# Shorter algebra at the two row ends, seven half-units kept, and a reload moved behind the last unit

## The reference

```python
# _gn: group norm, 32 groups of 16 channels, for each batch b and group g
x0 = x
v = (x - mean_group) / sqrt(var_group + 1e-5)
y1 = depthwise_conv(v, w1)            # w1 is H x 1: one value per (b, c, column), [b, c, 1, W]
y2 = depthwise_conv(v, w2)            # w2 is 1 x W: one value per (b, c, row),    [b, c, H, 1]
xl1 = relu(batchnorm(y1) * g1 + b1)   # mean and variance over both batches and the 256 values
xl2 = relu(batchnorm(y2) * g2 + b2)
dot[c, b] = sum_k xl1[b, c, k] * xl2[b, c, k]
num = dot.reshape(b, c)               # (512, 2) read as (2, 512): row 0 comes from channels 0..255
num = softmax((num @ lw1.T + lb1) @ lw2.T + lb2)
return x0 + v * num[:, :, None, None]
```

## Time and profile before

| what | value |
|---|---|
| median of 3 runs | 1709.55 us (1707.28 to 1709.72) |
| profiled execution: time | 1705.58 us |
| profiled execution: span | 1703.8 us |
| PE, DVE, ACT, POOL busy | 28%, 59%, 39%, 30% |
| DMA | 723.80 MB, mean 425 GB/s |
| HBM | 454.63 MB read, 268.44 MB written |

### The profile page before, as it was taken

The page is one execution under the profiler, slowest core; times in us unless marked ns, Lnnn a source line. Parts: engine busy times, 40 slices in busy tenths (PEclk is TensorE's granted clock), DMA queues, the critical chain, the costliest instruction groups (busy, mean ns, idle before and its releaser), DMA issues.

```text
span 1703.8 us, 14430 instructions
## 1 busy us (share of the span) xinstructions
PE 485.6 (28%) x3416; PEld 169.7 (10%) x3416; DVE 1004.7 (59%) x2672; ACT 665.1 (39%) x517; POOL 508.9 (30%) x489
## 2 busy tenths in 40 slices
PE   3588766660223321223333243430000000000000
PEld 1123212120001100001001021210000000000000
DVE  5899999967757576776666786772222222222220
ACT  4688887856435455544445546600000000000000
POOL 7678787820315444443254000000000000000000
PEclk8799878885666665666566566665555555555555
DMA  9999999989999999999999999999999999999999
GB/s 393 426 425 427 427 428 426 428 338 419 432 428 431 431 430 431 430 432 430 432 430 430 431 428 430 430 385 431 431 432 431 432 431 431 432 431 432 431 431 408
DMA packets 52126, 723.80 MB, mean 425 GB/s; under 512 B 6241, under 2 KB 6753, under 8 KB 8034
## 3 DMA queue, kind: packets, MB, share of 16 engines
q1 hardware_dynamic: 33922, 458.84, 63.4%
q10 hardware_dynamic: 18144, 264.25, 36.3%
HBM read 454.63 MB, written 268.44 MB: 424 GB/s over the span
## 4 chain that ended last, share of the span: by engine, by line
DMA 39%; another core or an unknown queue 26%; DVE 8%; PE 3%; issue 2%; ACT 2%; SPq 1%; DVEq 1%; POOL 0%; ACTq 0%; POOLq 0%
DMA xs<-in_x 28%; DMA out<-xs 11%; DVE xs L1104 3%; PE ps_part L576 2%; DVE xs L1028 1%; DVE mul_junk L1002 1%; DVE y2s L1031 1%; SPq L378 1%; ACT xs L878 1%; PE ps_part L710 1%; ACT sq_junk L805 1%; DVEq L1002 0%; DVE xs L1002 0%; POOL rstd_b L468 0%
## 5 line engine op out<-in xcount | busy, mean ns | idle before, releaser
L805 ACT ACTIVATE sq_junk<-xs 128x4096 fp8e5<-128x4096 f32 x128 | 463.1, 3618 | 203.9 <-DMA xs<-in_x 198.6
L576 PE MATMUL ps_part<-xs,filters 128*32 128x512 f32 x1856 | 290.8, 781 | 525.3 <-DMA xs<-in_x 516.2
L1104 DVE TENSOR_SCALAR xs<-xs,scale,shift 128x4096 f32<-128x4096 f32 x90 | 222.8, 2496 | 353.9 <-DMA xs<-in_x 353.3
L1002 DVE SCALAR_TENSOR_TENSOR xs<-xs,ps_w 128x256 f32 (+1 forms) x832 | 294.5, 416 | 28.6 <-DMA xs<-in_x 18.4
L534 POOL TENSOR_TENSOR xs<-xs,w_late 128x2048 f32<-128x2048 f32 x40 | 179.6, 4526 | 102.6 <-ACT w_late L819 102.6
L878 ACT ACTIVATE xs<-xs,shift,scale 128x4096 f32<-128x4096 f32 x33 | 125.3, 3798 | 157.3 <-DVE xs L1104 135.5
L576 PEld LDWEIGHTS ps_part<-xs,filters 128*32 128x32 f32 x1856 | 79.3, 138 | 718.3 <-issue 718.3
L1028 DVE TENSOR_TENSOR xs<-xs,ps_w 128x4096 f32<-128x4096 f32 x26 | 114.7, 4413 | 52.8 <-PE ps_part L576 46.6
L468 POOL TENSOR_TENSOR rstd_b<-var,minus_half 128x2 f32<-128x2 f32 (+1 forms) x23 | 15.2, 661 | 417.2 <-DVE var L1054 417.2
L1022 DVE TENSOR_REDUCE y2s<-xs 128x8 f32<-128x2048 f32 x40 | 91.4, 2286 | 77.1 <-POOL xs L534 77.1
L439 POOL TENSOR_TENSOR xs<-xs 128x768 f32<-128x768 f32 x64 | 116.7, 1827 | 58.0 <-DMA xs<-in_x 55.0
(11 more groups left out here) (116 smaller groups left out, 458.4 us busy)
## 6 DMA issues: line engine op xcount, KB each, us to landing
xs<-in_x SPq DMA_DIRECT2D x209, 2048.0 KB, 24.0
out<-xs ACTq DMA_DIRECT2D x121, 2048.0 KB, 27.6
filters<-in_x SPq DMA_DIRECT2D x5, 2048.0 KB, 18.0
out<-filters ACTq DMA_DIRECT2D x5, 2048.0 KB, 86.2
xs<-in_lw SPq DMA_DIRECT2D x2, 2048.0 KB, 16.3
out<-xs SPq DMA_DIRECT2D x2, 2048.0 KB, 12.1
filters<-in_w_rows SPq DMA_DIRECT2D x1, 512.0 KB, 3.8
filters<-in_w SPq DMA_DIRECT2D x1, 512.0 KB, 8.9
```

Source lines behind the costliest of these rows:

```text
L576: last = nc.tensor.matmul(ps_part[g % 2][32 * a:32 * a + 32, :], taps[:, g % 2, hf * JH + j, :], xs[:, s[0]:s[1] + 1:s[1] - s[0], j * W:(j ...
L805: nc.scalar.activation(sq_junk[:], xs[:, s, :], ACT.Square, accum_out=sq_sum[:, u % 2, u // 2, b:b + 1], saturate=False).then_inc(squared, 1)
L1002: return nc.vector.scalar_tensor_tensor(out=out, in0=x_row, scalar=1.0, in1=ps_w2[g % 2][:, 0:W], op0=ALU.mult, op1=ALU.mult, accum_out=total)
L1104: return nc.vector.tensor_scalar(buffer(s), buffer(s), scale[:, b, g:g + 1], shift[:, b, g:g + 1], ALU.mult, ALU.add)
```

## The change

It has six parts.

- (a) `HELD` goes from 6 to 7: seven half-units of batch 1 stay in SBUF, and 57 are read again. Unit 57 of batch 1 moves to slot 8.
- (b) The 28 reloads of batch 0 are handed out anew: steps 38, 43 and 48 get two, steps 55, 56, 59 and 61 none, and the last is loaded behind the last unit (slot 3) and scaled by ACT behind the last store of its batch.
- (c) The order of slots in stage 4 is 8, 9, 2, 6, 7, 4, 5, then FILTERS, 0, 1, 3, so the load into FILTERS stands first. It now also waits for the rows of the last half-unit, since DVE's rows of group 31, batch 1, write their unused output there (without waits between sets).
- (d) At the row ends, the last quad: `normalise`, `channel_moments`, `channel_factors` and `rectify` are replaced by `last_quad`, which takes moments of the raw sums for each batch and forms one scale and one shift from them with small DVE operations and two POOL powers (one of which runs beside the moments). One ACT pass makes the first factor, DVE makes the second, and the logits start with batch 0's dots.
- (e) The softmax: PE adds the logits into all 128 partitions at once (its weights are the dots, broadcast), so exponential and sum are made in every partition and the four transposes, the mask and the spreading product go.
- (f) In the last group before the first row end PE convolves each batch by itself; at both row ends `turn_rows` takes three of its four groups ahead of the last half-units; the moments come ahead of the fold; `keep_warm` is 6 in one piece instead of 3 and 2. POOL waits for the coefficients before it builds the next filters.

```diff
-HELD = 6
+HELD = 7
-REWORK_AT = list(range(FIRST + 1, UNITS - 6)) + [UNITS - 5, UNITS - 3]
+TWICE = (FIRST + 6, FIRST + 11, FIRST + 16)
+REWORK_AT = sorted([*range(FIRST + 1, UNITS - 9), *TWICE, UNITS - 7])
 def rework_slot(r):
-    if r < REWORK - 4:
+    if r < REWORK - 2:
         return (2, 3, 8)[(r - 2) % 3]
-    return (3, 8, 3, 8)[r - REWORK + 4]
+    return 3
 def last_slot(i):
-    return (9, 2, 6, 7, 4, 5, 3, 8, 0, 1, FILTERS)[i % S]
+    return (8, 9, 2, 6, 7, 4, 5, FILTERS, 0, 1, 3)[i % S]
...
+            load_again(REWORK - 1)              # SP, behind the last x load
             for i in range(HELD, UNITS):
...
                 elif s == FILTERS:
                     sp.wait_ge(pe_read_x, filters_before(UNITS - 1, 1))
+                    sp.wait_ge(rows_done, rows_before(UNITS - 1, 1) + SETS)
...
             def finish_row(row):
                 q = FQ * (row + 1) - 1
+                moments(batch_of(QG * (q + 1) - 1, 1))
                 fold_parts(QG * (q + 1) - 1)
-                moments(batch_of(QG * (q + 1) - 1, 1))
-                turn_rows(q)
-                pe.wait_ge(bn_ready, q + 1)
-                keep_warm(3)
+                turn_rows(q, range(QG - 1, QG))
+                keep_warm(6)
                 add_logits(q)
-                keep_warm(2)
-                spread_prob(row)
...
+            def rectify_last(row):
+                act.wait_ge(joint_ready, row + 1)
+                for b in range(B):
+                    half = slice(b * W, (b + 1) * W)
+                    nc.scalar.activation(z[:, half], ps_y1[:, half], ACT.Relu, scale=z_scale[:, 0, b:b + 1],
+                                         bias=z_shift[:, 0, b:b + 1]).then_inc(z_done, 2)
...
+                elif b and g == G - 1:          # DVE rows of group 31, batch 1
+                    for j in range(JH):
+                        last = row(last_junk[:, j], xs[:, s, j * W:(j + 1) * W], sums[:, j:j + 1])
+                    last.then_inc(rows_done, SETS)
...
+            def last_quad(row):
+                group_moments(k)                                    # then POOL: own_rstd = var ** -0.5
+                ...                                                 # own_off, 1 operation
+                    for b in range(B):
+                        last = nc.vector.bn_stats(bn_st2[:, B * i + b], y[:, b * W:(b + 1) * W])
+                ...                                                 # 4 bn_aggr, 10 operations of 2 or 4 columns
+                                               op0=ALU.add, op1=ALU.add).then_inc(spread_ready, 1)
+                ...                                                 # POOL: var_r = var_s ** -0.5, then 4 small operations
+                last.then_inc(joint_ready, 1)
+                for b in range(B):
+                    nc.vector.tensor_scalar(ps_y2[:, halves[b]], ps_y2[:, halves[b]], z_scale[:, 1, b:b + 1],
+                                            z_shift[:, 1, b:b + 1], ALU.mult, ALU.add).then_inc(y2_scaled, 1)
+                for b in range(B):
+                    nc.vector.scalar_tensor_tensor(
+                        out=z[:, halves[b]], in0=ps_y2[:, halves[b]], scalar=0.0, in1=z[:, halves[b]],
+                        op0=ALU.max, op1=ALU.mult, accum_out=dots[:, q, b:b + 1]).then_inc(dots_ready, 1)
...
             def softmax(row):
                 dve.wait_ge(logits_ready, row + 1)
-                nc.vector.reduce_max(neg_max[:], ps_l[0:1, :], AX.X, negate=True).then_inc(exp_asked, 1)
+                nc.vector.tensor_tensor(by_group, ps_l[:].rearrange("p (g c) -> p g c", c=CG),
+                                        own[:].unsqueeze(1).to_broadcast([P, G, CG]), ALU.mult)
+                nc.vector.reduce_max(neg_max[:], ps_l[:], AX.X, negate=True).then_inc(exp_asked, 1)
+                nc.vector.tensor_reduce(logit_g[:], by_group, AX.X, ALU.add).then_inc(logits_taken, 1)
                 dve.wait_ge(exp_done, row + 1)
...
             copy_parts(FG - 1)
-            normalise(FQ - 1)
-            rectify(FQ - 1)
+            rectify_last(0)
             exponential(0)
...
-            normalise(Q - 1)
-            rectify(Q - 1)
+            rework(REWORK - 1)
+            rectify_last(1)
             exponential(1)
```

More of the change, by code:

```diff
@@ L570, in convolve @@
                     if g >= 2:
-                        pe.wait_ge(part_copied, 2 * (g - 1))
+                        pe.wait_ge(part_copied, 2 * g if g in (FG - 1, FG) else 2 * (g - 1))
+                if u == FIRST - 1:
+                    turn_rows(FQ - 1, range(QG - 1))
+                if g == FG - 1:
+                    for b in range(B):
+                        pe.wait_ge(x_loaded[s[b]], landed(s[b], ("x", u, b)))
+                        for j in range(JH):
+                            a = j % 4
+                            last = nc.tensor.matmul(
+                                ps_part[b][32 * a:32 * a + 32, 0:W], taps[:, g % 2, hf * JH + j, :],
+                                xs[:, s[b], j * W:(j + 1) * W],
+                                start=(hf == 0 and j < 4), stop=(hf == 1 and j >= JH - 4))
+                    last.then_inc(pe_read_x, 1)
+                    return
                 for b in range(B):
@@ L614, in turn_rows @@
                 for e in range(E):
-                    for a in range(QG):
+                    for a in groups:
                         last = nc.tensor.matmul(
@@ L618, in turn_rows @@
                             sel[:, q % 2, e, :], y2s[:, (QG * q + a) % (2 * QG)], start=True, stop=True)
-                last.then_inc(y2_turned, 1)
+                if groups[-1] == QG - 1:
+                    last.then_inc(y2_turned, 1)
             def moments(k):
@@ L689, in add_logits @@
                         pe.wait_ge(exp_done, row)
-                    nc.tensor.matmul(ps_l[0:1, :], one[:], bias[:], start=True, stop=False)
-                pe.wait_ge(dots_ready, 2 * (q + 1))
+                        pe.wait_ge(logits_taken, row)
+                    nc.tensor.matmul(ps_l[:], one[:].to_broadcast([1, P]), bias[:], start=True, stop=False)
                 for b in range(B):
-                    last = nc.tensor.matmul(ps_l[0:1, :], dots[:, q, b:b + 1], mixed[:, B * h + b, :],
+                    pe.wait_ge(dots_ready, 2 * q + b + 1)
+                    last = nc.tensor.matmul(ps_l[:], dots[:, q, b:b + 1].to_broadcast([P, P]), mixed[:, B * h + b, :],
                                             start=False, stop=(q % FQ == FQ - 1 and b == B - 1))
@@ L775, in _ @@
                 if g % QG == 0 and g != FG:
[L776 removed]
+                    turn_rows(g // QG - 1, range(QG))
             for g in range(SPLIT, G):
@@ L1031, in multiply_rows @@
                     nc.vector.tensor_reduce(sums, x_rows, AX.X, ALU.add).then_inc(rows_done, SETS)
+                elif b and g == G - 1:
+                    dve.wait_ge(pe_read_x, filters_before(2 * g - 1, 1))
+                    dve.wait_ge(rows_done, before)
+                    for j in range(JH):
+                        last = row(last_junk[:, j], xs[:, s, j * W:(j + 1) * W], sums[:, j:j + 1])
+                    last.then_inc(rows_done, SETS)
                 else:
@@ new lines, in softmax, with coefficients @@
+                nc.vector.reduce_max(neg_max[:], ps_l[:], AX.X, negate=True).then_inc(exp_asked, 1)
+                dve.wait_ge(exp_asked, row + 1)
+                nc.vector.tensor_reduce(logit_g[:], by_group, AX.X, ALU.add).then_inc(logits_taken, 1)
+                dve.wait_ge(exp_done, row + 1)
+                then_wait(nc.vector.reciprocal(exp_sum[:], exp_sum[:]))
+                dve.wait_ge(powers_done, row + 1)
+            def coefficients(row, half):
+                if half == 0:
+                    of = [t[:, row, 0:FG].rearrange("p (q a) -> p q a", a=QG) for t in (scale, shift)]
+                    facts = [t[:, :, row:QG * B:B] for t in (rstd_a, nmr_a)]
+                    powers = logit_g[:, 0:FG].rearrange("p (q a) -> p q a", a=QG)
+                else:
+                    of = [t[:, row, FG:] for t in (scale, shift)]
+                    facts = [t[:, :, row] for t in (rstd_b, nmr_b)]
+                    powers = logit_g[:, FG:]
+                for t, fact in zip(of, facts):
+                    last = nc.vector.scalar_tensor_tensor(out=t, in0=fact, scalar=exp_sum[:], in1=powers,
+                                                          op0=ALU.mult, op1=ALU.mult)
+                return last
```

195 lines of the change are left out of this document (113 added, 82 removed).

## The result

| what | before | after |
|---|---|---|
| median | 1708.38 us (1705.9 to 1709.72, 6 runs) | 1716.33 us (1712.88 to 1717.07, 6 runs) |
| profiled execution: time, span | 1705.58, 1703.8 us | 1717.07, 1715.3 us |
| HBM read | 454.63 MB | 452.53 MB |

What follows compares the result with a forecast made beforehand. The kernel was taken as bound by its DMA engines almost everywhere, apart from holes at both row ends. 4.9 + 4.2 + 1.2 - 0.5 = 9.8 us off 1709.55 gave 1699.7, forecast as 1699.5 us; range 1693 to 1705.

Steps and rivals of the forecast that it cites:

- 4.2 us for the first row end: First row end: coefficients come 4.2 us earlier, at 363.5, so the hole of 8.7 us becomes 4.5; bounds 2.5 to 5.5.
- 1.2 us for the second: Second row end: 3 us of holes in place of 4.2; bounds all 4.2 gained or 4 us lost.
- 0.5 us charged for the doubled steps: Steps 38, 43 and 48: SP waits longer for reload stores, covered by loads in flight; 0.5 us for all three, bounds 0 to 6.
- one transfer less: Reloads of batch 1: 57 instead of 58 removes 4.87 us, sure as long as the holes do not grow.
- The first hole: Lost DMA time at the first row end, 8.7 us, said to end when the first scaled half-unit is stored.
- rival 2: Row ends: keep_warm(6) at the low clock holds back the logits, the 4.2 us gain goes at the first: 1704; chance 0.10.
- each us by which the coefficients come earlier is a us off the hole: First row end: the rule that turned coefficients 4.2 us earlier into 4.2 us less hole.
- Rival 5: The hole does not follow the coefficients; another wait ends it and only the saved transfer is left: 1704.7 us; chance 0.07.
- my bound of 35: Second reload of steps 38, 43 and 48: SP's wait for a reload's store is at most 10.6 + 24.4 = 35 us.
- DVE's 99 us against 97 us of transfers: Landing of (57, 1) to (63, 1): DVE's work and 20 transfers come out level, so the stretch loses its slack.
- rival 1: Second row end starves: DVE falls behind in groups 29 to 31, 5 us more of holes, 1706; chance 0.16.
- 0.03 to slower: Chance of a slower kernel: doubled steps starve the stream at steps 38, 43 and 48, up to 33 us of hole, 1732.

Runs made afterwards that it cites:

- The algebra alone: Parts (d), (e), (f) put on the kernel before, with its reloads, slots and load order unchanged: 1706.9 us, 0.9995 of before.
- the two delays: More dead matmuls in keep_warm at the first row end: 7 on the kernel before with (d), (e), (f), 1707.01 us; 12 on the kernel before, 1716.42 us.
- the two kernels that take away either half of the cause: Kernel after with one reload a step, 1703.63 us; kernel after with two rows instead of four per DVE set in groups 28 to 31, 1702.96 us.
- DVE lightened: Kernel after with two rows instead of four in each DVE set in groups 28 to 31, those row sums left out: 1702.96 us, 0.9967 of before.

## Why the prediction was wrong

Three terms of the sum failed: 4.2 us for the first row end was worth nothing that could be measured, 1.2 us for the second was a loss, and the 0.5 us charged for the doubled steps missed what they do to DVE.

- **What bounds the kernel.** The base holds: one transfer less is worth its bytes as long as nothing waits. "It is sure as long as the holes do not grow" was the right condition, and it failed.
- **The first hole: the step from coefficients to time failed.** The coefficients came as early as forecast and earlier (361.5 against 363.5). The 12 passes of `keep_warm` ran from 350.81 to 356.23, 0.45 us each, and the logits start at 356.42, so rival 2 does not hold at this end. But "all that was loadable has landed by about 361" was false: the last load landed at 372. And "each us by which the coefficients come earlier is a us off the hole" read the mean of 16 engines as if they were one. The earlier trace rows shows a share of 0.21 for 360 to 370; cut finer, it is 0.06 from 365 on, one engine working off what it still owes. Every half-unit is spread over the engines and landed only when the last has finished. Giving the other 15 work earlier lets them run ahead, and then they wait for the late one. The algebra alone gained nothing (0.9995), and the two delays place the line at about 371.5: nothing is lost up to 371.56, and 8.9 us (6.7 to 10.9 by the interval) back from 378.32 is 369.4 (367.4 to 371.6). Rival 5, to which I gave 0.07, had this mechanism, though not the time, since it left (b) and the second row end as they were. The Trainium skill (DMA: Bandwidth & Descriptors, Why a DMA increments its semaphore by 16 and not by 1) says that a transfer runs on up to 16 engines that finish independently, and that only the full count means that it has landed; the windows and the 16 signals above agree, and I had not used it.
- **The doubled steps: mis-sized.** I charged 0.5 us, for SP's wait alone. That wait did come (21.4 us at the most at L348, inside my bound of 35), but the cost is elsewhere. Three reloads and three stores moved ahead of the x loads are 6 x 4.87 = 29 us, and x comes later by that much: the first scaling of group 27 starts 31 us later. SP's wait was sized right; that x comes late behind it, and that DVE then has no slack to make it good, was put at nothing. The kernel before, then after:

```profile
937.76 3.30 DVE L1104 TENSOR_SCALAR xs<-xs,scale,shift 128x4096 f32<-128x4096 f32 x1
```

```profile
969.13 3.30 DVE L1200 TENSOR_SCALAR xs<-xs,scale,shift 128x4096 f32<-128x4096 f32 x1
```

- **The second row end: the wrong quantity was balanced.** I set DVE's 99 us against 97 us of transfers from one landing to another and expected a small hole. The transfers that were moved away from here no longer fill the stretch, and DVE begins it late with a full queue: its scaling of group 28 starts at 1008.31, 23 us behind the 985.12 of the kernel before. From there to the end of the last rows at 1115.58 it needs 107 us and never waits for data. Its next scalings start at 1035.53, 1069.60 and 1102.01, which is 21, 14 and 8 us late: it catches up, but not in time. The DMA engines have too little to do instead: 324, 318, 212 and 242 GB/s in the windows above. This is rival 1's mechanism (DVE falls behind, the stores of batch 0 come late, SP holds the loads), with its price too low: I priced 5 us more of holes. Counting the hole at the first end as no loss before or after, the rest is 7.7 (measured) + 4.9 (the transfer saved) = 12.6 us, and the two kernels that take away either half of the cause give 12.7 and 13.4 us back. The windows of the profiled executions fit: of the 21.8 us more that 900 to 1150 lacks, 5.5 are the lead of the first hole given back, and the 16.3 left are the 11.5 us of span and the 4.9 of the transfer. FILTERS "can go when the last rows are done" was true, and may have turned against the change: its load waits 29.9 us for them (L394) with all other loads of the stage behind it. What that wait costs by itself was not measured. With DVE lightened it is still 19.6 us, in a kernel that is faster than the one before.
- **`keep_warm` at the second end.** Here the 12 passes do hold back the logits, from 1117.54 to 1123.71. It does not matter for the time that was lost: they stand behind the late rows.

The forecast gave 0.03 to slower. What made it so sure was a ledger whose entries were added as if they were independent; (b) and the DVE count were two sides of one thing. The sign of being wrong that it named, a rate under 428 GB/s in stage 3, did appear.

## What to carry to other kernels

Where the DMA share stands near 1/16, an earlier restart of the other engines need not gain anything: cut the window finely, see whether one engine is still at its full rate, and count the time only from where the share is 0.00. When transfers are moved earlier, write down what now arrives later and which engine must then work it off without slack; balance that engine's work against the time from its new start, not against the bytes that are left. Keep deferrable transfers for the stretch in which an engine is the limit.

## What the runs showed of the hardware

One DMA engine ran some 8 us behind the other 15 after 360 us of load near the full rate: they stopped at about 363.5 and it at 372.0, in two kernels whose TensorE programs differ by 1024 instructions. It fell behind steadily, by 1.8 us on average between 100 and 150 us and by 7.2 between 300 and 350. Where the hole was too short to catch up, the lag stayed at about 6 us for over 500 us. The 1024 instructions cost 4 packets of 16 KB on queue q8 (31 against 27), and no time that could be measured.
